# FFN stage: h divided by its scale on GpSimd, with Silu, the residual sum and the root chain reordered

## The reference, cut to what matters

```python
def fp4_quant_dequant(x):              # BLOCK = 16, along the last dimension
    xb = x.reshape(shape[:-1] + (shape[-1] // BLOCK, BLOCK))
    scale = jnp.maximum(jnp.max(jnp.abs(xb), -1, keepdims=True) / 6.0, 1e-12)
    xn = xb / scale
    idx = jnp.searchsorted(_MID, jnp.abs(xn))      # to 0, .5, 1, 1.5, 2, 3, 4, 6
    return (_GRID[idx] * jnp.sign(xn) * scale).reshape(shape)

gate = fp4_linear(x, w_gate)           # 256 -> 704
y = fp4_linear(x, w_up)                # 256 -> 704
h = jax.nn.silu(gate) * y
out = layernorm(x + fp4_linear(h, w_down))         # 704 -> 256
```

## Time and profile before

| | us |
|---|---|
| median of 3 executions | 673.51 (673.32 to 674.2) |
| the profiled execution | 673.45 |
| its span | 671.5 |
| VectorE busy in the span | 580.9 |
| TensorE busy in the span | 588.0 |
| ScalarE, GpSimd busy | 335.6, 187.3 |

### The profile page before, as it was taken

The page is one execution under the profiler, slowest core; times in us unless marked ns, Lnnn a source line. Parts: engine busy times, 40 slices in busy tenths (PEclk is TensorE's granted clock), DMA queues, the critical chain, the costliest instruction groups (busy, mean ns, idle before and its releaser), DMA issues.

```text
span 671.5 us, 14647 instructions
## 1 busy us (share of the span) xinstructions
PE 588.0 (88%) x4290; PEld 502.6 (75%) x4290; DVE 580.9 (87%) x1439; ACT 335.6 (50%) x869; POOL 187.3 (28%) x230
## 2 busy tenths in 40 slices
PE   3179999999999999999999677779988999999965
PEld 2158888788787878788787566669877888888755
DVE  6056889999999999999998779989999999999996
ACT  3125656666575666666575643224434334433332
POOL 1011124334533444334530203232222222222110
PEclk9779999999999999999999798979999999999998
DMA  6471101110111001110110000000000000000001
GB/s 155 55 230 41 32 25 49 47 39 8 47 47 47 23 23 47 47 39 8 47 31 18 8 8 2 1 0 19 28 16 16 16 16 16 16 16 16 17 16 48
DMA packets 25853, 23.11 MB, mean 34 GB/s; under 512 B 2024, under 2 KB 22760, under 8 KB 25832
## 3 DMA queue, kind: packets, MB, share of 16 engines
q1 hardware_dynamic: 25016, 21.27, 11.3%
q10 hardware_dynamic: 816, 1.57, 0.7%
HBM read 17.56 MB, written 5.28 MB: 34 GB/s over the span
## 4 chain that ended last, share of the span: by engine, by line
DVE 23%; PE 18%; issue 9%; ACT 1%; POOL 1%; DVEq 1%; ACTq 0%; POOLq 0%
PE wide_banks L1182 9%; PE upd_y L1182 5%; DVE shared L800 2%; DVE stats L926 2%; DVE shared L922 2%; DVE shared L993 1%; PE wide_banks L1340 1%; DVE h_amax L782 1%; DVE shared L989 1%; DVE win_lo L913 1%; DVE shared L795 1%; DVE win_lo L910 1%; DVE h_inv L791 1%; DVE h_scale L787 1%; POOL shared L1160 1%
## 5 line engine op out<-in xcount | busy, mean ns | idle before, releaser
L1160 POOL TENSOR_TENSOR shared<-shared,h_scale 128x704 f32<-128x704 bf16 x32 | 44.4, 1387 | 202.5 <-DVE shared L805 196.9
L1182 PE MATMUL wide_banks<-wgu_hi,xq_hi 128*128 128x512 f32 (+1 forms) x192 | 65.1, 421 | 27.8 <-DVE xq_lo L982 27.8
L1182 PE MATMUL wide_banks<-win_hi,x_hi 128*128 128x512 f32 x192 | 68.5, 438 | 12.9 <-DVE win_lo L885 11.0
L442 ACT ACTIVATE shared<-opened,rstd 128x64 f32<-128x64 f32 x256 | 64.7, 335 | 11.0 <-DVE rstd L715 10.7
L413 ACT ACTIVATE shared<-shared 128x704 bf16<-128x704 f32 x32 | 25.3, 790 | 83.4 <-DVE shared L795 83.4
L1241 PEld LDWEIGHTS mixed<-shared 128*128 128x128 f32 x512 | 62.0, 192 | 2.8
L1182 PE MATMUL wide_banks<-win_hi,x_lo 128*128 128x512 f32 x192 | 60.8, 398 | 0.0
L1182 PE MATMUL wide_banks<-win_lo,x_hi 128*128 128x512 f32 x192 | 60.8, 398 | 0.0
L1241 PE MATMUL mixed<-shared 128*128 128x64 f32 x512 | 60.6, 271 | 0.0
L1182 PEld LDWEIGHTS wide_banks<-wgu_hi,xq_hi 128*128 128x128 f32 x192 | 33.1, 200 | 36.0 <-DVE xq_lo L982 33.0
L1182 PE MATMUL wide_banks<-wgu_hi,xq_lo 128*128 128x512 f32 (+1 forms) x192 | 58.9, 389 | 0.0
(11 more groups left out here) (146 smaller groups left out, 1496.3 us busy)
## 6 DMA issues: line engine op xcount, KB each, us to landing
xf<-in_x_feat SPq DMA_DIRECT2D x32, 128.0 KB, 2.2
tab<-in_tables SPq DMA_DIRECT2D x16, 256.0 KB, 2.7
xt<-in_x_tok SPq DMA_DIRECT2D x32, 128.0 KB, 2.1
out<-shared SPq DMA_DIRECT2D x32, 128.0 KB, 1.7
x<-in_w_in ACTq DMA_DIRECT2D x3, 512.0 KB, 5.3
w<-in_w_gu SPq DMA_DIRECT2D x1, 1408.0 KB, 7.8
pow_dram<-powers SPq DMA_DIRECT2D x1, 1056.0 KB
w<-in_w_down SPq DMA_DIRECT2D x1, 704.0 KB, 9.1
```

The costliest lines, as they stand in the source:

```text
L442: last = act.activation(gated[:, b, cols], opened[:, b, cols], ACT.Copy, scale=rstd[:, b, 1 + k:2 + k])
L1160: pool.tensor_tensor(over_blocks(hq[:, b]), over_blocks(h_steps[:, b]), spread(h_fp4["scale"][:, b]), ALU.mult).then_inc(h_fp4["ready"], 1)
L1182: last = pe.matmul(dst, lhs, rhs, start=k == 0, stop=k == len(parts) - 1)
```

## The change

Four things change in the FFN bodies. `h_to_unit` goes from VectorE to the head of GpSimd's body, ahead of `rescale_x`, and there multiplies h with an inverse that already has sign and rounding factor in it: so `h_scale` gets a second operation on the maximum, which writes the negative divisor, and `h_inverse` takes the reciprocal of that in place. ScalarE opens the second Silu part ahead of the size pass. VectorE does the residual sum first in every body, where bodies with b = 1 did it behind the division. And the root chain's square goes behind the first up product, the four steps after it behind the second.

```diff
--- before.py
+++ after.py
@@ -543,10 +543,10 @@
                     split_xq(n + 1, 1 - b)
                 if valid(n - 3):
                     split_h(n - 3, 1 - b)
+                if valid(n):
+                    open_ffn(n, 1)
                 if valid(n - 1):
                     size_h(n - 1, 1 - b)
-                if valid(n):
-                    open_ffn(n, 1)
                 if valid(n - 5) and b == 0:
                     norm_out(n - 6, 0)
                     norm_out(n - 5, 1)
@@ -784,16 +784,13 @@
             def h_scale(n, b):
                 need(dve, h_fp4["ready"], n - 1)
                 dve.wait_ge(h_fp4["step"], H_STEPS * n + 1)
-                dve.tensor_scalar(h_fp4["scale"][:, b], h_fp4["amax"][:], 1.0 / FP4_MAX, SCALE_MIN, ALU.mult, ALU.max).then_inc(h_fp4["step"], 1)
+                dve.tensor_scalar(h_fp4["scale"][:, b], h_fp4["amax"][:], 1.0 / FP4_MAX, SCALE_MIN, ALU.mult, ALU.max)
+                dve.tensor_scalar(h_fp4["inv"][:], h_fp4["amax"][:], -TIE_DOWN / FP4_MAX, -SCALE_MIN * TIE_DOWN,
+                                  ALU.mult, ALU.min).then_inc(h_fp4["step"], 1)
 
             def h_inverse(n, b):
                 dve.wait_ge(h_fp4["step"], H_STEPS * n + 2)
-                dve.reciprocal(h_fp4["inv"][:], h_fp4["scale"][:, b]).then_inc(h_fp4["step"], 1)
-
-            def h_to_unit(n, b):
-                dve.wait_ge(h_fp4["step"], H_STEPS * n + 3)
-                dve.scalar_tensor_tensor(over_blocks(h_unit[:, b]), over_blocks(h), -1.0 / TIE_DOWN, spread(h_fp4["inv"][:]),
-                                         ALU.mult, ALU.mult).then_inc(h_fp4["step"], 1)
+                dve.reciprocal(h_fp4["inv"][:], h_fp4["inv"][:]).then_inc(h_fp4["step"], 1)
 
             def h_shift(n, b):
                 dve.wait_ge(h_fp4["rounder_ready"], n + 1)
@@ -1002,8 +999,8 @@
                 out, quant, norm = valid(n - 5), valid(n - 1), valid(n - 5) and b == 0
                 last = n - 5
                 done = pair_done(last)
-                if norm:
-                    add_out(n - 5, 1)
+                if out:
+                    add_out(n - 5, 1 - b)
                 if quant:
                     for at in h_done:
                         dve.wait_ge(at, n)
@@ -1019,33 +1016,24 @@
                     h_inverse(n - 1, 1 - b)
                 if norm:
                     pair_var(done)
-                if quant:
-                    h_to_unit(n - 1, 1 - b)
-                if norm:
                     pair_guess(done)
-                elif out:
-                    add_out(n - 5, 0)
                 if valid(n + 1):
                     split_xq(n + 1, 1 - b)
-                if norm:
-                    pair_square(done)
-                elif out:
+                if out and not norm:
                     out_stats(n - 5, 0)
                 if valid(n - 3):
                     split_h0(n - 3, 1 - b)
+                    split_h1(n - 3, 1 - b)
+                if valid(n):
+                    gate_up0(n)
+                if norm:
+                    pair_square(done)
+                if valid(n):
+                    gate_up1(n)
                 if norm:
                     pair_product(done)
-                if valid(n - 3):
-                    split_h1(n - 3, 1 - b)
-                if norm:
                     pair_fine(done)
-                if valid(n):
-                    gate_up0(n)
-                if norm:
                     pair_fine_square(done)
-                if valid(n):
-                    gate_up1(n)
-                if norm:
                     pair_fine_product(done)
                 if quant:
                     h_shift(n - 1, 1 - b)
@@ -1154,12 +1142,20 @@
                 need(pool, xT_done, n - 1)
                 pool.tensor_tensor(over_blocks(xq[:, b]), over_blocks(x_steps[:, n]), spread(x_scales[:, n]), ALU.mult).then_inc(xq_ready, 1)
 
+            def h_to_unit(n, b):
+
+                pool.wait_ge(h_fp4["step"], H_STEPS * n + 3)
+                need(pool, h_fp4["rounded"], n - 1)
+                pool.tensor_tensor(over_blocks(h_unit[:, b]), over_blocks(h), spread(h_fp4["inv"][:]), ALU.mult).then_inc(h_fp4["step"], 1)
+
             def rescale_h(n, b):
                 need(pool, hT_done, n - 1)
                 pool.wait_ge(h_fp4["rounded"], n + 1)
                 pool.tensor_tensor(over_blocks(hq[:, b]), over_blocks(h_steps[:, b]), spread(h_fp4["scale"][:, b]), ALU.mult).then_inc(h_fp4["ready"], 1)
 
             def ffn_body(n, b):
+                if valid(n - 1):
+                    h_to_unit(n - 1, 1 - b)
                 if valid(n + 2):
                     rescale_x(n + 2, b)
                 if valid(n - 1):
```

More of the change, by code:

```diff
@@ L1035, in ffn_body @@
                     split_h0(n - 3, 1 - b)
-                if norm:
-                    pair_product(done)
-                if valid(n - 3):
                     split_h1(n - 3, 1 - b)
-                if norm:
-                    pair_fine(done)
                 if valid(n):
@@ L1044, in ffn_body @@
                 if norm:
-                    pair_fine_square(done)
+                    pair_square(done)
                 if valid(n):
@@ L1048, in ffn_body @@
                 if norm:
+                    pair_product(done)
+                    pair_fine(done)
+                    pair_fine_square(done)
                     pair_fine_product(done)
```

## The result

The changed kernel took 650.12 us (649.75 to 651.12, 4 runs) against 673.66 us before (4 runs): ratio 0.9652, interval 0.9635 to 0.9669, some 23.5 us less. The forecast was 669.6 with a range of 660 to 679.

A forecast was written before the change was run, and what follows sets the result against it. VectorE was taken as the bound; bodies without root chain gain 0.65 us, those with it lose 0.32: -4.3 us over 13 pairs, +0.2 first tiles, +0.3 last, total -3.8 from 673.45 to 669.6 us; range 660 to 679.

The forecast's parts named there:

- the price of the division: FFN bodies, GpSimd: the moved division of h, 704 columns, takes 1.84 us, scaled from the weights' rescaling.
- The estimate of 1.53 us by the Trainium skill: GpSimd's division at about 2.6 cycles an element at 1.2 GHz; would put the sum at 661.5 us.
- Case (a): Rival: GpSimd's division is cheap, 1.39 to 1.65 us; middle gives 661.3 us, 1.39 gives 657.9; chance 0.13.
- the long square of 0.3 us: Root chain on VectorE: the square waits for GpSimd's rescaling of x and lasts 0.3 us or so.
- The hand-over to GpSimd in O: Body without root chain: GpSimd starts the division 0.14 us after VectorE releases it.
- the first five tiles: First quantised tiles, without sum and statistics: each loses 0.04 us, five of them 0.2 us.
- TensorE's reserve: FFN tiles: TensorE works 7.16 us a tile and has about 0.7 us (0.74) in reserve.
- TensorE has no idle time left: Sign in the profile after the change that would show the prediction wrong.
- the place of the new wait: VectorE ahead of the first gate product: idle 0.5 to 0.6 us until GpSimd's division is done.
- the sum hidden in O: Body without root chain: the residual sum, 0.33 us, moved first, hides in the scale's wait for GpSimd.
- the lost race: Rival, body with root chain: GpSimd starts before the guess, which waits the whole division; 683.5 us; chance 0.13.
- Case (d): Rival: the change does nothing, since the division was hidden on VectorE; no chance given.

The follow-up runs named there:

- run 7: Changed kernel with f32 and bfloat16 products on GpSimd alone added behind its end; whole about 35 us longer, f32 spread product of 704 columns 1.385 us.
- Run 6: Changed kernel with a 192-column product put ahead of the division on GpSimd; 666.02 us, ratio 0.9877 to the kernel before.
- Run 1: Changed kernel with the division alone put back on VectorE, ahead of the root chain's guess; 677.30 us, ratio 1.0051 to the kernel before.
- run 10: Changed kernel with scale behind the reciprocal in bodies without root chain, and ahead of the statistics' wait in bodies with it; 645.73 us, ratio 0.9591.
- run 9: Changed kernel with the scale computed before the wait for the statistics in bodies with root chain; 647.28 us, ratio 0.9612.
- run 3: Changed kernel with the residual sum again behind the reciprocal in bodies without root chain; 656.52 us, ratio 0.9713.
- run 2: Changed kernel with ScalarE's size pass again ahead of the second Silu part; 685.00 us, ratio 1.0162 to the kernel before.
- run 5: Changed kernel with the root chain's guess moved behind the x split, so GpSimd's division has begun; 661.45 us, ratio 0.9811.
- runs 4: Changed kernel with the root chain's square, product and following steps again spread between splits and products; 657.12 us, ratio 0.9748.
- runs 8: Changed kernel with divisor first and scale behind the reciprocal in bodies without root chain; 649.65 us, ratio 0.9643.

## Why the prediction was wrong

**The step that failed** is the price of the division: "The like f32 operation over blocks of 16, the rescaling of weights, took 1.01 us for 352 columns; with the same fixed part, 704 columns take 0.18 + 2 x 0.83 = 1.84 us." It measured 1.39 us. The row had 0.22 us of waiting in it (run 7), and doubling it doubled the wait too: 1.84 less twice 0.22 is 1.40. The other end of the bounds, "1.39 us if f32 input costs nothing", was the truth to 0.01 us. By the prediction's own rate (2.6 us for each 0.1 over 13 pairs) this step is 11.7 of the 19.5 us by which the forecast missed. Run 6 shows the same from the other side: 1.87 us of GpSimd work brings the time back to 666, 14.5 us up from the 651.6 of the changed kernel.

The estimate of 1.53 us by the Trainium skill ("GPSIMD Engine Reference", 3.1 Elementwise) was set aside in favour of the row. It was nearer, though for a product without a spread operand the trace has 1.667.

**What the rest is.** Case (a) at 1.39 us was given as 657.9, 15.5 us less; the span became 22.2 us shorter, 6.7 more than that. The pair was to be 14.57 and is 14.25. Three terms of it are off, 0.28 of the 0.32 us. The second product comes 0.49 us behind the first (503.98 to 504.47), where 0.64 was reckoned: the square starts at 504.39 and ends at 504.54, GpSimd's rescaling at 504.52, so that wait fell into the square's own length, and the long square of 0.3 us that the prediction named as a sign did not come. The hand-over to GpSimd in O is 0.08 us (509.96 to 510.04), not 0.14; in E it is 0.16. And the division in E starts 2.68 us into the body, not 2.75. Over the stretch of 13 pairs the gain is 19.15 us, where (a) had 13 x 1.23 = 16.0. The other 3.5 us lie outside it: the first five tiles were to lose 0.2 and gained 2.9, less the 0.56 of the later start, and the end was to lose 0.3 and gained 0.7. Of the first tiles' share 5 x 0.45 = 2.25 us comes from the same price, as run 6 bears out. Run 1, with the division on VectorE, still has 1.3 of their 2.9 us (49.09, from 50.39), so some of it comes with the new order; that was not taken apart.

**TensorE's reserve** was mis-sized too, without bearing on the forecast. It was read as 7.16 us of work a tile, and case (a) made 2 x 7.16 = 14.32 us a pair "nearly the bound"; the pair of 14.25 is already below that, and tiles that follow without idle time start 6.86 us apart. Before, they start 7.86 to 7.94 us apart, so the reserve was 1.0 us a tile, not 0.7. And "TensorE has no idle time left", named as a sign of being wrong, came true from 455 to 517 us, and in run 10 from 453 us to the end of the steady part, and in neither was TensorE the bound.

**What held.** VectorE as the bound before (though its pair was not "without gaps": 0.23 us of idle time stands ahead of the scale in E, which run 9 takes away); the place of the new wait, ahead of the first product; the second operation on the maximum at 0.09 us (509.33 + 0.17 against 509.18 + 0.23); the sum hidden in O (run 3); Silu's order as a condition for the gain (run 2); the blocked scale in E set free; the root steps in a row; the place of the lost race, and that it costs the whole rest of the division (run 5); TensorE's new wait for the rescaling of x. Case (d) is refuted by run 1 as well. O now begins 0.10 us behind the rounding's end (507.83), where it used to overlap it by 0.08, hidden by the scale's wait. This is the forecast wait for ScalarE's norm output: VectorE's sequencer is through the wait for it at 507.77, just behind the end of its first half (507.72), then spends until 507.88 on a register operation for the next wait. In the body behind the loop (sum at 621.65), where the code has the wait but not the register operation, the sum overlaps the rounding by 0.08 us again.

The chance of 0.13 for case (a), with 0.54 on a window of 5 us, was too sure for a price that had two rows at its ends and nothing in between to decide.

## What to carry to other kernels

Before the length of an instruction is scaled up, look at what the other engines do during it: a wait of GpSimd for VectorE, or the other way round, stands inside the length (runs 4, 5 and 7), and in a loop that runs in step it is the same every time, so that a small spread proves nothing. When work moves to an idle engine and the receiver's wait becomes part of the critical loop, every queue that the result passes counts: here the move was worth 26 us (run 1 against the changed kernel) with Silu ahead of the size pass, and less than nothing behind it (run 2, 685.0 against 674.3 us). And once a loop closes over two engines, one operation or one wait less on the path is worth about its length in each body (runs 8 to 10), however short. An engine without idle time need not be the bound: it can be one that is behind and catching up (TensorE here).

## What the hardware showed that I had not expected

- GpSimd multiplies f32 as fast as bfloat16: 1.385 and 1.382 us for 704 columns (run 7).
- A spread operand makes the product cheaper: 1.385 against 1.667 us for 704 columns, 0.786 against 0.925 for 352.
- A VectorE operation on two elements can last 1.31 us (run 5) or 1.06 us (run 4), and GpSimd's instructions can hold 0.22 us of waiting in turn.
